# A state-space layer and its feed-forward part: part of the turns of x and the sum of squares leave TensorE

## The chip, the cores and the metric

The kernel runs on one core of a Trainium2 chip. The metric is the device time of one execution in microseconds (us); the lower the better. Its median over three runs is 1739.33 us.

## What is computed

The input is x, two sequences of 512 tokens with 512 features. A Mamba-2 layer and then a gated feed-forward layer with LoRA terms are added to it. What matters here is the scan of the first, which the reference runs in chunks (cut; the kernel takes chunks of 128 tokens and not of 32, with the same result):

```python
proj = input_states @ in_proj_w.T                     # gate, x, B, C, dt
xBC = silu(conv(xBC) + conv_b)                        # 4 taps along the tokens
scores = einsum('bcihn,bcjhn->bcijh', Cc, Bc) * Ldec * dtc
y_intra = einsum('bcijh,bcjhp->bcihp', scores, xc)
states = einsum('bcjh,bcjhn,bcjhp->bchpn', dtc * dlast, Bc, xc)
y_inter = einsum('bcihn,bchpn->bcihp', Cc * exp(cum), prev)
y = y_intra + y_inter + Dp * x
g = y * silu(gate)
gg = g.reshape(b, l, G, GS)                           # 8 groups of 1024 channels
var = mean(gg * gg, axis=-1)
g = (gg * rsqrt(var + EPS)).reshape(b, l, INTER) * norm_w
return g @ out_w.T
```

Two things of this are touched. `y_intra` and `states` sum over tokens, so they need x with the tokens on the partitions, while the projection leaves it with the channels there: x is turned. And `var` is a mean over 1024 channels, which lie on the partitions (8 tiles of 128), so its last step is a sum across partitions.

## The kernel before

It is written by hand for five engines, each with its own program and semaphores between them. There are 8 groups of 16 heads (1024 channels) and, in each, 8 chunks of 128 tokens (4 to a sequence): 64 slots, one for each group g and chunk k. K counts them, c = k mod 4 is the place in the sequence.

In one slot TensorE (PE) does, in this order: `inside` (L1788, decay times x, 32 matmuls); `square_total` (L1862, the sum of squares of the slot before, y times a column of ones); `new_state` (6 matmuls, on L1712 to L1714); the first projection tile of the next unit; `turn_x` (L1762, eight 128x128 transposes of x of the next chunk, through PSUM); `match` (L1771, L1772); `across` (L1803, 16 matmuls), which writes PSUM in which y of this chunk lies until DVE has gated it; two more tiles; `out_half`; a tile; `out_half`; the last tile. A tile of the projection is 12 matmuls of 512 columns (L1712 to L1714). Where c = 3 there is no new state and no `across`, and there are three tiles and not five.

VectorE (DVE) adds the skip to y (L1436), adds the new state (L1473, L1475), adds epsilon to the sum of squares (`mean_square`, L1481), gates (`gated`, L1449), runs the convolution's taps for finished tiles (L1385), scales x by dt out of PSUM into xdt (`scale_x`, L1404), accumulates the output of the slot before (L1487), scales `across` (L1425), and multiplies the scores (L1415). In slot k = 0 of a group it also makes the low halves of the output weights (`ow_low`, L1391). GpSimd (POOL) makes low halves (w_l L704, gT_l L738, xw_l L733), masks (L710), weighs x (`weigh_x`, L725), adds up squares within a partition (L744 to L748) and takes the inverse root (L753). ScalarE (ACT) drains, activates and squares. SyncE (SP) issues every DMA, in the order of its program, and waits where a buffer isn't free; all of them go to one queue.

What sets the order is the order in which each engine's program is written; nothing is scheduled. A PE matmul on a tile i waits until tile i - 2 has been drained and convolved, since two PSUM banks take turns. `scale_x` of the next chunk stands on DVE behind the gating and the first taps, and `accumulate` behind it.

```python
# DVE before
dve.wait_ge(ss_done, K + 1)
dve.tensor_scalar(mean_sq[:, :], total_of(K), EPS, None, ALU.add).then_inc(mean_ready, 1)
# PE, across
pe.wait_ge(g_half, K)
pe.wait_ge(state_ready, n_state(g, k))
```

## Time and profile before

| what | value |
|---|---|
| median of three runs | 1739.33 us (1739.27 to 1741.21) |
| span of the profiled execution, first to last instruction | 1737.2 us |
| granted TensorE clock over it | 0.999 of full speed |
| PE busy | 1724.5 us, 99% |
| DVE busy | 1221.0 us, 70% |
| ACT busy | 1192.8 us, 69% |
| POOL busy | 1182.1 us, 68% |
| DMA | 211.63 MB, queue of SP 41.7% of 16 engines' span |

The profile lists the span of its execution; the time around it is not listed apart, and the median run is 2.1 us above the span. A span is the time from the first to the last instruction; busy time is the time in which an engine computes. An average over the span hides that the slots differ: those with c = 3 take 17 us, the others 25.6 us, and DVE is nearly full in the first two slots of a group.

### The profile page before, as it was taken

The page shows a single profiled execution, that of the slowest core. Times are in us where ns is not written, and L with a number is a line of the kernel's source. Part 1 is how long each engine was busy: PE and PEld are TensorE (multiplying, and loading weights), DVE is VectorE, ACT ScalarE, POOL GpSimd, SP SyncE. Part 2 cuts the span into 40 slices and gives each one's busy share as a digit, 9 for nine tenths or more (in the row PEclk, how much of TensorE's full clock was granted, in tenths as well). Part 3 has the DMA queues.
Part 4 walks back from the last instruction along what each step waited for, and adds up shares of the span by engine and source line. Part 5 has one row for each costly group of instructions (what it writes and reads, how often), then busy time and mean ns, then how long its engine had stood idle before and what let it go on. Part 6 is the DMA issues. An engine that isn't in the chain of part 4 may idle for free.

```text
span 1737.2 us, 27735 instructions
## 1 busy us (share of the span) xinstructions
PE 1724.5 (99%) x9925; PEld 1436.9 (83%) x9925; DVE 1221.0 (70%) x2154; ACT 1192.8 (69%) x2232; POOL 1182.1 (68%) x1058
## 2 busy tenths in 40 slices
PE   9999999999999999999999999999999999999999
PEld 7788888888888888888888888888888888787887
DVE  8886778768785769676875878586867688663323
ACT  6887677767867677767776777768777777663421
POOL 5586768677777668676867687766867686774510
PEclk9999999999999999999999999999999999999999
DMA  5534435343543443443534354345343353444201
GB/s 192 171 107 116 125 116 169 109 119 105 162 128 114 121 146 112 121 116 112 174 115 115 97 162 128 114 122 151 114 118 113 110 174 101 118 114 134 80 15 49
DMA packets 122056, 211.63 MB, mean 122 GB/s; under 512 B 24256, under 2 KB 28992, under 8 KB 121920
## 3 DMA queue, kind: packets, MB, share of 16 engines
q1 hardware_dynamic: 121920, 209.87, 41.7%
q8 instruction: 80, 1.31, 0.3%
q14 instruction: 56, 0.46, 0.1%
HBM read 205.09 MB, written 4.72 MB: 121 GB/s over the span
## 4 chain that ended last, share of the span: by engine, by line
PE 97%; DVE 1%; DMA 1%; POOL 0%; ACT 0%; issue 0%; POOLq 0%
PE bank L1712 19%; PE bank L1714 18%; PE bank L1713 18%; PE bank L1788 7%; PE bank L1846 7%; PE bank L1836 7%; PE bank L1829 7%; PE bank L1803 5%; PE bank L1762 2%; PE bank L2091 1%; PE bank L2092 1%; PE bank L2093 1%; PE bank L1862 1%; PE bank L1772 1%; PE bank L1953 1%; DMA w_raw<-in_wp 0%
## 5 line engine op out<-in xcount | busy, mean ns | idle before, releaser
L704 POOL TENSOR_TENSOR w_l<-w_raw,w_h 128x512 fp32r<-128x512 f32 x288 | 379.6, 1321 | 341.2 <-ACT w_h L900 341.2
L1712 PE MATMUL bank<-x_h,w_h 128*128 128x512 f32 (+1 forms) x1328 | 527.0, 397 | 3.9 <-DVE x_ch L1385 2.3
L1714 PE MATMUL bank<-x_h,w_l 128*128 128x512 f32 (+1 forms) x1328 | 519.7, 391 | 0.0
L1713 PE MATMUL bank<-x_l,w_h 128*128 128x512 f32 (+1 forms) x1328 | 518.1, 390 | 0.0
L1385 DVE SCALAR_TENSOR_TENSOR x_ch<-bank,par,x_ch 128x511 f32<-128x511 f32 (+2 forms) x384 | 287.2, 749 | 80.3 <-ACT x_ch L918 71.2
L953 ACT ACTIVATE decay<-decay,cols 128x128 f32<-128x128 f32 x1024 | 318.2, 390 | 3.7 <-DMA cdec<-cdec_scratch 1.6
L1712 PEld LDWEIGHTS bank<-x_h,w_h 128*128 128x128 f32 (+1 forms) x1328 | 249.5, 188 | 55.1 <-issue 3.1
L1714 PEld LDWEIGHTS bank<-x_h,w_l 128*128 128x128 f32 (+1 forms) x1328 | 249.2, 188 | 54.6
L1713 PEld LDWEIGHTS bank<-x_l,w_h 128*128 128x128 f32 (+1 forms) x1328 | 249.7, 188 | 51.1
L1415 DVE TENSOR_TENSOR decay<-decay,bank 128x512 f32<-128x512 f32 x256 | 171.3, 683 | 107.1 <-ACT decay L953 107.1
L918 ACT ACTIVATE x_ch<-bank,par 128x512 f32<-128x512 f32 x128 | 99.0, 774 | 185.6 <-PE bank L1714 185.5
L710 POOL TENSOR_SCALAR_AFFINE_SELECT decay<-decay 128x512 f32<-128x512 f32 x256 | 173.9, 697 | 65.8 <-DMA decay<-cum_scratch 64.3
L1436 DVE SCALAR_TENSOR_TENSOR bank<-x_ch,par,bank 128x128 f32<-128x128 f32 x512 | 138.4, 350 | 92.8 <-PE bank L1788 92.8
L900 ACT ACTIVATE w_h<-w_raw 128x512 fp32r<-128x512 f32 x288 | 178.7, 621 | 4.4 <-DMA w_raw<-in_wp 4.4
L738 POOL TENSOR_TENSOR gT_l<-sgT,gT_h 128x1024 fp32r<-128x1024 f32 x64 | 153.9, 2405 | 8.2 <-ACT gT_h L972 8.2
L939 ACT ACTIVATE sgT<-bank 128x512 f32<-128x512 f32 x122 | 71.9, 590 | 111.9 <-PE bank L1714 111.7
L1846 PE MATMUL bank<-ow_h,gT_h 128*128 128x512 f32 x512 | 137.3, 390 | 0.0
L1836 PE MATMUL bank<-ow_h,gT_l 128*128 128x512 f32 x512 | 136.9, 389 | 0.0
L1829 PE MATMUL bank<-ow_l,gT_h 128*128 128x512 f32 x512 | 136.9, 389 | 0.0
L1788 PEld LDWEIGHTS bank<-decay,xdt 128*64 128x64 f32 x2048 | 110.5, 137 | 22.6 <-issue 22.6
L1788 PE MATMUL bank<-decay,xdt 128*64 128x128 f32 x2048 | 125.9, 276 | 0.0
L733 POOL TENSOR_TENSOR xw_l<-xw,xw_h 128x1024 fp32r<-128x1024 f32 x48 | 114.9, 2394 | 0.3 <-ACT xw_h L965 0.3
(161 smaller groups left out, 2760.0 us busy)
## 6 DMA issues: line engine op xcount, KB each, us to landing
w_raw<-in_wp SPq DMA_DIRECT2D x288, 256.0 KB, 3.0
decay<-cum_scratch SPq DMA_DIRECT2D x256, 256.0 KB, 4.1
ec<-ecum_scratch SPq DMA_DIRECT2D x96, 256.0 KB, 6.2
ow_raw<-in_ow SPq DMA_DIRECT2D x64, 256.0 KB, 4.8
w_raw<-in_w SPq DMA_DIRECT2D x48, 256.0 KB, 2.7
acc<-in_x SPq DMA_DIRECT2D x8, 256.0 KB, 4.5
out<-acc SPq DMA_DIRECT2D x8, 256.0 KB, 2.0
cols<-cols_scratch SPq DMA_DIRECT2D x16, 96.0 KB, 2.7
```

Of the source, the lines that this page charges most:

```text
L704: pool.tensor_tensor(w_l[:, s, :], w_raw[:, s, :], w_h[:, s, :].bitcast(F32), ALU.subtract).then_inc(wl_ready, 1)
L710: pool.affine_select(out=d, in_=d, compare_op=ALU.is_ge, fill=fill, base=0, pattern=[[0, QH], [1, P]], channel_multiplier=-1).then_inc(mas ...
L900: act.activation(w_h[:, s, :], w_raw[:, s, :], ACT.Copy).then_inc(wh_ready, 1)
L953: last = act.activation(decay[:, h, :], decay[:, h, :], ACT.Exp, bias=cols[:, b, CUM, c, h:h + 1], scale=-1.0)
L1385: dve.scalar_tensor_tensor(out=conv(bu, t)[:, s:], in0=bank_of(u, i)[:, 0:SEQ - s], scalar=w, in1=conv(bu, t)[:, s:], op0=ALU.mult, op1=AL ...
L1712: pe.matmul(dst, wh, xh, start=(opens and k == 0), stop=False)
L1713: pe.matmul(dst, wh, xl, start=False, stop=False)
L1714: last = pe.matmul(dst, wl, xh, start=False, stop=(k == len(terms) - 1 and not more))
L1788: last = pe.matmul(yb[n // 4][a * HDIM:(a + 1) * HDIM, tok(n % 4)], xdt[:, h * HDIM:(h + 1) * HDIM], decay[:, h, :], start=(c == 0), stop= ...
L1829: last = pe.matmul(ob[:, :], gT_h[:, n, :], ow_l[:, n, :], start=False, stop=(k == 0 and n == CT - 1))
L1836: last = pe.matmul(ob[:, :], gT_l[:, n, :], ow_h[:, n, :], start=False, stop=(k > 0 and n == CT - 1))
L1846: pe.matmul(ob[:, :], gT_h[:, n, :], ow_h[:, n, :], start=(n == 0), stop=False)
```

## The change

For chunks with c > 0 (three in four) PE no longer turns x. DVE turns it in 32x32 blocks into a spare buffer (`ec_sq` for c = 1, `xw_sq` for c = 2 and 3, in the space of ec and xw). Four DMAs put the blocks in their places in a scratch in DRAM (`store_x`), and one brings the turned chunk back into `x_rows` (`fetch_x`), in the space of gT_l. DVE's turns stand in slots c = 1 (for c = 3) and c = 3 (for c = 2 and c = 1 of the next unit). `scale_x` then reads `x_rows` in SBUF. Since `x_rows` lies under gT_l, POOL's gT_l waits for `scale_x`; since `xw_sq` lies under xw, POOL's `weigh_x` waits for the store. The fetch is the first DMA of its slot (behind par, cols and cdec where c = 0).

The sum of squares no longer goes to PE. At the head of the next slot DVE turns the 128x128 partial squares in blocks, sums each block over its 32 columns, and turns the 128x32 result (`turn_squares`); four DMAs of 4 rows of 128 bytes move it from SBUF to SBUF (`move_squares`, behind the second decay load); DVE turns what has arrived, sums 4 values and adds epsilon (`mean_square`), now behind `gated` and not ahead of it.

```diff
 def scale_x(g, k):                                   # DVE
-    dve.wait_ge(tx_done, K + 1)
+    if c > 0:
+        dve.wait_ge(x_fetched, 16 * moved_no(K))
+    else:
+        dve.wait_ge(tx_done, K // SC + 1)
...
+    xs = x_rows.rearrange("p (a s n t) -> p a n s t", a=2, s=QUADS // 2, n=CT)
...
+        last = dve.tensor_tensor(xd[:, a, :, :, :], xs[:, a, :, :, :], by, ALU.mult)
+def turn_x(g, k):                                    # DVE
...
+    dve.transpose(x_sq_of(k).rearrange("p b n t -> p n b t"), x_ch[:, b, :, tok(c)]).then_inc(x_turned, 1)
 def mean_square(g, k):                               # DVE
-    dve.wait_ge(ss_done, K + 1)
-    dve.tensor_scalar(mean_sq[:, :], total_of(K), EPS, None, ALU.add).then_inc(mean_ready, 1)
+    dve.wait_ge(sq_moved, 16 * QUADS * (K + 1))
+    dve.transpose(sq_back[:, :], sq_full[:, :]).then_inc(mean_step, 1)
+    dve.wait_ge(mean_step, 2 * K + 1)
+    dve.tensor_reduce(mean_sq[:, :], sq_back[:, 0:QUADS], mybir.AxisListType.X, ALU.add).then_inc(mean_step, 1)
+    dve.wait_ge(mean_step, 2 * K + 2)
+    dve.tensor_scalar(mean_sq[:, :], mean_sq[:, :], EPS, None, ALU.add).then_inc(mean_ready, 1)
+def turn_squares(g, k):                              # DVE
+    dve.wait_ge(sum_ready, K + 1)
+    dve.transpose(y[:, 1, :], y[:, 0, :]).then_inc(sq_turned, 1)
+    dve.wait_ge(sq_turned, K + 1)
+    dve.tensor_reduce(sq_part[:, 0:QUADS], y[:, 1, :].rearrange("p (b t) -> p b t", b=QUADS), ...)
+    dve.wait_ge(sq_summed, K + 1)
+    if some(K):
+        dve.wait_ge(sq_moved, 16 * QUADS * K)
+    dve.transpose(sq_rows[:, :], sq_part[:, :]).then_inc(sq_flipped, 1)
+def store_x(g, k):                                   # SP
+    sp.wait_ge(x_turned, turned_no(K))
+    for q in range(QUADS):
+        sp.dma_start(dst[q], x_sq_of(k)[q * SQ:(q + 1) * SQ, :, :, :]...).then_inc(x_stored[K % 2], 16)
+def fetch_x(g, k):                                   # SP
+    sp.wait_ge(x_stored[K % 2], stored_no(K))
+    if some(K - 1):
+        sp.wait_ge(out_done, 2 * (K - 1))
+    sp.dma_start(x_rows[:, :], xt_dram[K % 2]).then_inc(x_fetched, 16)
+def move_squares(g, k):                              # SP
+    sp.wait_ge(sq_flipped, K + 1)
+    if some(K):
+        sp.wait_ge(mean_ready, K)
+    for q in range(QUADS):
+        sp.dma_start(sq_full[q:P:SQ, :], sq_rows[q * SQ:q * SQ + QUADS, :]).then_inc(sq_moved, 16)
 def weigh_x(g, k):                                   # POOL
+    if c == 2:
+        pool.wait_ge(x_stored[1], stored_no(K + 1))
...
+    elif c == 0 and some(K):
+        pool.wait_ge(x_stored[0], stored_no(K + 2))
 def gT_low(g, k):                                    # POOL
+    if c < SC - 1:
+        pool.wait_ge(xdt_ready, K + 2)
-def square_total(g, k):                              # PE
-    pe.wait_ge(sum_ready, K + 1)
-    pe.matmul(total_of(K), y[:, 0, :], ones[:, :], start=True, stop=True).then_inc(ss_done, 1)
```

On DVE, at the start of slot k = 0 of a group, the order before is this (ow_l are the output weights' low halves, xdt is what `scale_x` writes, sgT what `gated` writes):

```order
L1436 SCALAR_TENSOR_TENSOR bank<-x_ch,par,bank 128x128 x8
L1475 COPY state<-bank 128x512 x2
L1481 TENSOR_SCALAR mean_sq<-bank 128x1
L1449 TENSOR_TENSOR sgT<-bank,sgT 128x4x128 x2
L1391 SCALAR_TENSOR_TENSOR ow_l<-ow_raw,par,ow_h 128x512 x2
L1404 TENSOR_TENSOR xdt<-bank,cols 128x512 x2
L1487 SCALAR_TENSOR_TENSOR acc<-bank,rstd,acc 128x512
```

And after the change, from the same place:

```order
L1607 STREAM_TRANSPOSE y<-y 128x128
L1609 TENSOR_REDUCE sq_part<-y 128x4
L1614 STREAM_TRANSPOSE sq_rows<-sq_part 128x32
L1552 SCALAR_TENSOR_TENSOR bank<-x_ch,par,bank 128x128 x8
L1591 COPY state<-bank 128x512 x2
L1565 TENSOR_TENSOR sgT<-bank,sgT 128x4x128 x2
L1597 STREAM_TRANSPOSE sq_back<-sq_full 128x32
L1599 TENSOR_REDUCE mean_sq<-sq_back 128x1
L1601 TENSOR_SCALAR mean_sq<-mean_sq 128x1
L1483 SCALAR_TENSOR_TENSOR ow_l<-ow_raw,par,ow_h 128x512 x2
L1509 TENSOR_TENSOR xdt<-x_rows,cols 128x8x64 x2
L1620 SCALAR_TENSOR_TENSOR acc<-bank,rstd,acc 128x512
```

Three instructions stand ahead of the skip (L1552), and three in place of one behind the gating; the ow_l, the scaling of x and the accumulation are queued behind them.

On SP, at the start of slot k = 0 of a group, before:

```order
L472 DMA par<-in_par 128x66
L475 DMA cols<-cols_scratch 128x192
L476 DMA cdec<-cdec_scratch 128x64
L455 DMA w_raw<-in_wp 128x512
L469 DMA ow_raw<-in_ow 128x512 x2
L481 DMA decay<-cum_scratch 128x512 x4
L487 DMA ec<-ecum_scratch 64x1024 x2
```

And after:

```order
L501 DMA par<-in_par 128x66
L504 DMA cols<-cols_scratch 128x192
L505 DMA cdec<-cdec_scratch 128x64
L534 DMA x_rows<-xt_scratch 128x1024
L484 DMA w_raw<-in_wp 128x512
L498 DMA ow_raw<-in_ow 128x512 x2
L510 DMA decay<-cum_scratch 128x512 x2
L545 DMA sq_full<-sq_rows 4x32 x4
L510 DMA decay<-cum_scratch 128x512 x2
L516 DMA ec<-ecum_scratch 64x1024 x2
```

The fetch of 512 KB stands ahead of the weights and decays, and the four moves of squares between the second and third decay load.

## Rows read from the trace of the kernel before

**Rows 1.** The page: busy time of the engines

```profile
PE 1724.5 (99%) x9925; PEld 1436.9 (83%) x9925; DVE 1221.0 (70%) x2154; ACT 1192.8 (69%) x2232; POOL 1182.1 (68%) x1058
```

**Rows 2.** Windows, slots 0, 1, 5 of group 4: PE, PEld, DVE, ACT, POOL

```profile
828.00:853.60 25.60, 25.60 (x154) 21.51 (x153) 23.15 (x35) 20.97 (x42) 21.76 (x17) 1.00 0.61 190
853.60:879.20 25.60, 25.60 (x154) 21.51 (x153) 22.74 (x40) 19.43 (x35) 20.91 (x18) 1.00 0.41 114
947.40:973.00 25.60, 25.60 (x152) 21.52 (x151) 20.81 (x36) 17.29 (x34) 18.31 (x16) 1.00 0.45 114
```

**Rows 3.** Timeline, DVE, slots 0, 1 and 3

```profile
834.26 1.41 DVE L1391 SCALAR_TENSOR_TENSOR ow_l<-ow_raw,par,ow_h 128x512 fp32r<-128x512 f32 x2
835.58 1.28 DVE L1404 TENSOR_TENSOR xdt<-bank,cols 128x512 f32<-128x512 f32 x2
837.62 0.75 DVE L1487 SCALAR_TENSOR_TENSOR acc<-bank,rstd,acc 128x512 f32<-128x512 f32 x1 [0.75 <-POOL rstd L753]
838.28 5.28 DVE L1391 SCALAR_TENSOR_TENSOR ow_l<-ow_raw,par,ow_h 128x512 fp32r<-128x512 f32 x4
...
855.84 2.16 DVE L1436 SCALAR_TENSOR_TENSOR bank<-x_ch,par,bank 128x128 f32<-128x128 f32 x8
...
859.16 1.28 DVE L1449 TENSOR_TENSOR sgT<-bank,sgT 128x512 f32<-128x512 f32 x2
...
908.14 1.29 DVE L1449 TENSOR_TENSOR sgT<-bank,sgT 128x512 f32<-128x512 f32 x2
```

**Rows 4.** Timeline, PE, slots 1 and 4: start us, length us

```profile
855.48 0.38 PE L1862 MATMUL bank<-ones,y 128*128 128x1 f32 x2
855.72 0.48 PE L1712 MATMUL bank<-xw_h,b_tok_h 128*128 128x512 f32 x1
...
859.94 0.80 PE L1762 MATMUL bank<-ident_r,x_chr 128*128 128x128 f32 x8
860.57 0.25 PE L1771 MATMUL bank<-ident_r,bcTr 128*128 128x128 f32 x1
...
860.95 1.95 PE L1803 MATMUL bank<-bcT,state 128*128 128x128 f32 x16
...
923.96 0.48 PE L1712 MATMUL bank<-xw_h,b_tok_h 128*128 128x512 f32 x1
```

**Rows 5.** Groups by line: busy us, mean ns of one

```profile
L1762 PE MATMUL bank<-ident_r,x_chr 128*128 128x128 f32 x512 | 51.1, 244 | 0.0
...
L1458 DVE TENSOR_TENSOR state<-state,cdec 128x1024 f32<-128x1024 f32 x32 | 46.2, 1445 | 0.0
...
L1412 DVE TENSOR_TENSOR b_tok_l<-bank,b_tok_h 128x128 fp32r<-128x128 f32 x64 | 18.0, 281 | 0.0
```

**Rows 6.** Timeline, decay loads issued by SP, slots 0 and 3

```profile
830.60 2.16 SPq L481 DMA_DIRECT2D decay<-cum_scratch  x4
...
905.49 1.75 SPq L481 DMA_DIRECT2D decay<-cum_scratch  x4
```

**Rows 7.** DMA issues, window 830.55 to 831.05 us

```profile
decay<-cum_scratch SPq DMA_DIRECT2D x1, 256.0 KB, 5.2
```

**Rows 8.** DMA issues, window 831.05 to 831.5 us

```profile
decay<-cum_scratch SPq DMA_DIRECT2D x1, 256.0 KB, 5.4
```

**Rows 9.** DMA issues, window 914.0 to 914.3 us

```profile
par<-in_par SPq DMA_DIRECT2D x1, 33.0 KB, 2.5
```

**Rows 10.** DMA issues, window 828.65 to 828.9 us

```profile
cdec<-cdec_scratch SPq DMA_DIRECT2D x1, 32.0 KB, 4.5
```

**Rows 11.** DMA issues of the whole span

```profile
ecum_scratch<-x_ch SPq DMA_DIRECT2D x4, 128.0 KB, 3.4
...
cdec_scratch<-cdecT SPq DMA_DIRECT2D x2, 2.0 KB, 3.7
```

**Rows 12.** Timeline, POOL, slot 3

```profile
916.51 1.91 POOL L725 TENSOR_TENSOR xw<-xdt,cols 128x1024 f32<-128x1024 f32 x1
...
921.00 2.38 POOL L733 TENSOR_TENSOR xw_l<-xw,xw_h 128x1024 fp32r<-128x1024 f32 x1
```

More of the change, by code:

```diff
@@ L33 @@
 PIECE = KT * P
+SQ = 32
+QUADS = P // SQ
 SLOT_TILES = [[("g", 0), ("g", 1), ("c", 0), ("c", 1), ("g", 2)],
@@ L129, in build @@
     cols_dram = nc.dram_tensor("cols_scratch", (GROUPS, BATCH, P, UNIT_COLS), F32, kind="Internal").ap()
+    xt_dram = nc.dram_tensor("xt_scratch", (2, P, GCH), F32, kind="Internal").ap()
     cdec_dram = nc.dram_tensor("cdec_scratch", (BATCH, GROUPS, GH * SC), F32, kind="Internal").ap()
@@ L174, in build @@
         decay = sc("decay", [P, GH, P])
+        ec_sq = under("ec_sq", [P, QUADS, CT, SQ])
         ec = sc("ec", [P, CT, P])
@@ L178, in build @@
         xw = under("xw", [P, GCH])
+        xw_sq = under("xw_sq", [P, QUADS, CT, SQ])
         xw_l = sc("xw_l", [P, GCH], F32R)
@@ L182, in build @@
         y_r = sc("y_r", [P, CT, P], F32R)
-        gT_h, gT_l = sc("gT_h", [P, CT, P], F32R), sc("gT_l", [P, CT, P], F32R)
+        gT_h = sc("gT_h", [P, CT, P], F32R)
+        x_rows = under("x_rows", [P, GCH])
+        gT_l = sc("gT_l", [P, CT, P], F32R)
         b_tok_h, b_tok_l = sc("b_tok_h", [P, P], F32R), sc("b_tok_l", [P, P], F32R)
@@ L326, in build @@
         tx_done = sem("tx_done")
+        x_turned = sem("x_turned")
+        x_stored = [sem(f"x_stored{n}") for n in range(2)]
+        x_fetched = sem("x_fetched")
         mt_done = sem("mt_done")
@@ L644, in body @@
                             load_decay(gn, kn, q)
+                            if q == 1 and some(K):
+                                move_squares(*before)
+                    if c == 0:
+                        sp.wait_ge(x_stored[1], stored_no(K + 1))
                     if more and kn % SC > 0:
@@ L655, in body @@
                         load_next_w(g, last, b, tiles[0])
+                    if c == 1 or first:
+                        store_x(g, k + 2)
+                    if c == SC - 1:
+                        store_x(gn, kn + 2)
                     if k == 0 and not first:
@@ L724, in weigh_x @@
                     pool.wait_ge(cols_stored[1], 32)
+                if c == 2:
+                    pool.wait_ge(x_stored[1], stored_no(K + 1))
+                elif c == 1 and not some(K - 1):
+                    pool.wait_ge(x_stored[0], stored_no(K + 1))
+                elif c == 0 and some(K):
+                    pool.wait_ge(x_stored[0], stored_no(K + 2))
                 pool.tensor_tensor(per_head(xw[:, :]), per_head(xdt[:, :]), spread(cols[:, b, ELAST, c, :], HDIM),
@@ L1402, in scale_x @@
                         dve.wait_ge(xw_ready, n_state(*((g, k) if k else (g - 1, CHUNKS))))
-                for h in range(2):
-                    last = dve.tensor_tensor(per_head(xdt[:, half(h)]), per_head(xt[h][:, :]),
-                                             spread(cols[:, b, DT, c, h * 8:h * 8 + 8], HDIM), ALU.mult)
-                last.then_inc(xdt_ready, 1)
+                if c == 0:
+                    for h in range(2):
+                        last = dve.tensor_tensor(per_head(xdt[:, half(h)]), per_head(xt[h][:, :]),
+                                                 spread(cols[:, b, DT, c, h * 8:h * 8 + 8], HDIM), ALU.mult)
+                    last.then_inc(xdt_ready, 1)
+                    return
+                xs = x_rows.rearrange("p (a s n t) -> p a n s t", a=2, s=QUADS // 2, n=CT)
+                xd = xdt.rearrange("p (n a s t) -> p a n s t", n=CT, a=2, s=QUADS // 2)
+                dts = cols[:, b, DT, c, :].rearrange("p (n a) -> p a n", a=2)
+                for a in range(2):
+                    by = dts[:, a, :].unsqueeze(2).unsqueeze(3).broadcast_to([P, CT, QUADS // 2, SQ])
+                    last = dve.tensor_tensor(xd[:, a, :, :, :], xs[:, a, :, :, :], by, ALU.mult)
+                last.then_inc(xdt_ready, 1)
+            def turn_x(g, k):
+                K, b, c = g * CHUNKS + k, k // SC, k % SC
+                dve.wait_ge(silu_done, conv_no(2 * g + b, CONV_TILES))
+                if c == 1 and some(K - 1):
+                    dve.wait_ge(z_scaled, n_across(g, k))
+                if c == 2:
+                    dve.wait_ge(st_done, n_state(g, k - 2) if some(K - 2) else 1)
+                if c == SC - 1:
+                    dve.wait_ge(st_done, n_state(g, k - 1))
+                dve.transpose(x_sq_of(k).rearrange("p b n t -> p n b t"), x_ch[:, b, :, tok(c)]).then_inc(x_turned, 1)
             def scores(g, k, q):
@@ L1583, in last_chunk @@
                 add_state(LAST, k)
+                gated(LAST, k)
                 mean_square(LAST, k - 1)
-                gated(LAST, k)
+                if k == SC + 1:
+                    turn_x(LAST, k + 2)
                 if k < CHUNKS - 1:
@@ L1630, in body @@
                         norm_apply(1, 1)
+                    if not first:
+                        turn_squares(*before)
                     if k != 1:
@@ L1639, in body @@
                         add_state(g, k)
+                        gated(g, k)
                         mean_square(*before)
-                        gated(g, k)
+                    if c == 1 or first:
+                        turn_x(g, k + 2)
+                    if c == SC - 1:
+                        turn_x(gn, kn + 2)
                     if late:
@@ L2028, in body @@
                         projects(tiles[2:3])
-                    if not first:
-                        square_total(*((g, k - 1) if k else (g - 1, CHUNKS - 1)))
                     new_state(g, k)
```

89 lines of the change are left out of this document (66 added, 23 removed).

## The prediction

> **What bounds the kernel now.** I read the page first. PE is busy for 1724.5 of 1737.2 us [rows 1], so the time is what PE has to do, and what leaves PE is a gain as long as nothing new makes it wait. Then the windows over slots of group 4, in mid-kernel, which show how much room the others have. In slot 0 of group 4, PE works 25.60 of 25.60 us at full granted clock (1.00, the 2.4 GHz level), DVE 23.15 and POOL 21.76; in slot 1 DVE 22.74 [rows 2]. In the fullest of the other slots, slot 5, DVE works 20.81. So the reader should look at DVE in the first two slots of a group: 5.3 us are free in two slots of 51.2 us, and the change gives DVE work there and takes time from PE there. The timeline of DVE in these slots [rows 3] shows that the room isn't where it would help: between the accumulation at 837.62 and the skip at 855.84 no row of it has an idle time.
>
> **What leaves PE.** Eight transposes of x take from 859.94 to 860.57, when the next kind of matmul begins: 0.63 us [rows 4]. There are 512 of them before [rows 5], 64 chunks of 8; three chunks in four leave, so 48 x 0.63 = 30.2 us. The sum of squares is one matmul in two passes for each of 64 chunks; from its start at 855.48 to that of the next matmul at 855.72 are 0.24 us [rows 4], and without it the next one starts in its place: 64 x 0.24 = 15.4 us. Together 45.6 us, which is the floor: 1739.3 - 45.6 = 1693.7 us.
>
> **What DVE gets.** The trace has no block transpose and no such reduction. The turn of x (128x1024) makes 1024 elements a partition, like the fading of the state, which takes 1.445 us in the mean with POOL beside it [rows 5]; a 128x512 one takes 0.64 (half of the 1.28 of the pair at 835.58 [rows 3]). I take 1.25 us, since one input is lighter than two; the bounds are 0.65 and 1.45. Turning the 128x128 squares I put at the 0.28 us of the 128x128 subtraction [rows 5], the reduction the same, the small turn at 0.15: 0.75 us at the head of each slot with what lies between them (bounds 0.4 and 0.85). The three small ones of `mean_square` I put at 0.5 us where there was one of 0.15 (bounds 0.3 and 0.85, three times the 0.28). `scale_x` from SBUF I leave at its 1.28 us (below for the other case). In the slots k = 2, 4, 5, 6 all this fits: the store and the fetch lie a slot ahead of their use, and DVE has at least the 4.8 us of slot 5 free there [rows 2]. There PE keeps the whole gain.
>
> **Where it doesn't fit: slot 0 and slot 1.** `mean_square` now waits for four tiny DMAs, and DVE waits in order, with ow_l, `scale_x`, `accumulate` and all of the slot behind it. When do these rows land? SP issues the decay loads of slot 0 from 830.60 on [rows 6]. The first lands after 5.2 us, at 835.8 [rows 7], the second, issued at 831.1, after 5.4, at 836.5 [rows 8], though a load alone lands far sooner: par, 33 KB, takes 2.5 us at 914.1 [rows 9]. What delays it is what stands ahead in the queue, and a small transfer isn't spared: cdec, 32 KB, took 4.5 us behind four loads of output weights [rows 10]. The moves are issued behind the second decay load, so they land behind it. The fetch, 512 KB, is now ahead of all: two times the 0.7 us between the two decay landings, 1.4 us. So the squares are there at 836.5 + 1.4 = 837.9, say 838.0.
>
> By the Trainium skill (DMA: Bandwidth & Descriptors, Queues, rings and completion order) each DMA engine works through the descriptors of a ring in ring order, so rows of 128 bytes stand behind the 256 KB loads on the engines that they use; the trace agrees, by cdec above.
>
> From 838.0: `mean_square` to 838.5; two ow_l, 1.41 [rows 3], to 839.9; `scale_x`, 1.28, to 841.2. `accumulate`, which began at 837.62, begins at 841.2: 3.6 us late. DVE then runs without a gap to the skip of slot 1, at 855.84 before, and three new instructions (0.75) stand ahead of it. So gating comes 4.35 us late. Its first half ended at 859.16 + 0.64 = 859.80 [rows 3]; it ends at 864.15. `across` waits for that half. It began at 860.95 [rows 4]; with two turns and two sums gone from the two slots, 1.74 us, it could begin at 859.2. PE therefore loses 4.95, say 5.0 us in slots 0 and 1 together. Part of it will show earlier, at the last tile of slot 0 (which waits for taps that now come 3.6 us late) and at gT_l, which waits for `scale_x`; these are the same 5.0 us, not more of them. Behind the gating the order holds: gated, `mean_square`, turn, taps end at 864.8 + 0.5 + 1.25 + 2.3 = 868.9, which is just when PE wants that bank. Seven groups have such a slot 0 (group 0 has no squares to move in it): 7 x 5.0 = 35 us. In slot 1 of group 0 DVE is as full; I put 1 us there.
>
> **Slots 3 and 7.** `weigh_x` there waits for the store of the turned c = 2. Gating ends at 908.14 + 1.29 = 909.4 [rows 3]. The decays are issued from 905.49, 0.44 us each [rows 6], so the last move goes out at about 907.7 and lands, at the 2.5 us of par in a quiet queue [rows 9], at 910.2. `mean_square` to 910.7, turn to 911.95, the last of four stores out at 913.3. A store of 128 KB lands in 3.4 us [rows 11]: 916.7, where `weigh_x` began at 916.51. Then squares and xw_l follow on POOL, which ended at 923.38 [rows 12] for a `new_state` that began at 923.96 [rows 4] and would now begin at 923.48. So of the 0.2 us about 0.1 to 0.2 shows, in 15 such slots 2 to 3 us; I take 3.
>
> **The sum.** 45.6 - 35 - 1 - 3 = 6.6 us gained. The profiled span of 1737.2 would be 1730.6, and the median of the runs, 2.1 us above that span, 1739.3 - 6.6 = 1732.7: I say 1733 us. A change can be told from none here from about 0.2%, 3.5 us, so this is a small gain, 0.4%. Its own range: with the fetch hidden (moves land at 836.5) the term of 35 falls by 7 x 1.4 = 10, to 1723; with the small instructions at their upper bounds (0.1 and 0.35 more on the path of 7 slots, the turn 0.2) it grows by 4.5, and with late stores by some more, to 1742.
>
> **Rivals.** *First, faster: the moved rows aren't held up.* They then land 2.5 us after the last issue, 833.3: 835.8. `mean_square` to 836.3, ow_l 837.7, `scale_x` 839.0: 1.4 us late, with the squares 2.15, `across` loses 2.75, 19 us in seven groups: 1739.3 - 45.6 + 19 + 4 = 1717 us. For it: the moves touch 16 rows in all, and that so small a transfer waits as cdec did isn't shown for them. Against it: cdec itself. If DVE catches up by shorter instructions too, the way leads on towards the floor, 1694. Chance 0.22.
>
> *Second, slower: the store of slots 3 and 7 is late.* If the moves take the 3.7 us of the 2 KB store of cdec [rows 11] and not 2.5, everything behind them in that slot is 1.2 us later, and the store lands at 917.9: `weigh_x`, xw_l and `new_state` are 1.4 us late, less the 0.1 of room, 15 x 1.3 = 20 us, in place of the 3: 1750 us. Every further microsecond (the store took 3.4 in a head with little traffic) costs 15 more. It turns the gain into a loss from 0.45 us of mean lateness above what I took. For it: DVE, SP, DMA and POOL stand in one row with no room in it. Against it: it needs both landings at their longer values. Chance 0.22.
>
> *Third, no change: `scale_x` from SBUF is slower.* Two ow_l at 834.26 take 1.41 us, four at 838.28 take 5.28, 1.32 each [rows 3]: the first while POOL waits, the others beside POOL's gT_l and masks. The new `scale_x` has both inputs in SBUF as they have, and may take 2.6 and not 1.28. In slot 0 that is 1.3 us more on the path, 7 x 1.3 = 9 us: 1742 us. Against it: in slot 0 POOL has nothing to do just then, since gT_l waits for this very instruction. Chance 0.14.
>
> The Trainium skill has this as a rule (VectorE: DVE Perf Modes, Two Vector instructions with no wait between them): what a Vector instruction with two SBUF inputs reads through the second SBUF read interface is shared with GpSimd. The trace agrees by the 1.32 against 0.70 us of the same instruction.
>
> **How the numbers follow.** The forecast's case has 0.42, of which 0.27 lies under 1735.8, 0.10 within 3.5 us of before and 0.05 above. The first rival is all faster (0.22), the second all slower (0.22), the third half within and half above (0.07 each). Faster: 0.27 + 0.22 = 0.49; same: 0.10 + 0.07 = 0.17; slower: 0.05 + 0.22 + 0.07 = 0.34. The range reaches into both outer rivals, from 1704 to 1755, and leaves 0.1 out on each side.
>
> **What would show it.** In the profile after: PE's rows have no L1762 in three chunks of four and 5.7 us less work a group; where my sum holds, a group takes about as long as before less 1 us, slots 2, 4, 5, 6 are 24.7 us, and slots 0 and 1 together 54.5 us less the gain they have in them, 1.74, plus 5.0, that is about 3.3 us longer than their 51.2. PE waits in them for DVE's taps and gating. On DVE in slot 0 there is an idle time of about 4 us ahead of the new `mean_square`, put down to the DMA of sq_full, and its landing is 6 us or so behind its issue. In the first rival this idle time is under 2 us. In the second, `weigh_x` in slots 3 and 7 waits for the DMA on xt_scratch and `new_state` for xw_l. In the third the pair of `scale_x` takes over 2 us. I would be most wrong if PE hardly waited anywhere, or if every slot waited for its squares and not slot 0 alone.

## The result, and the profile after

The changed kernel took 1757.97 us in the median (1754.29 to 1760.57, 4 runs), the kernel before 1739.3 (1739.09 to 1741.21, 4 runs): ratio 1.0104, interval 1.0092 to 1.0116. It is 18.7 us slower. The forecast was 1733, range 1704 to 1755, so it was wrong in sign and the time lies outside its range. The profiled run took 1760.57 us, with a span of 1758.8.

The engines' busy times on the page of the changed kernel:

```profile
PE 1697.5 (97%) x9413; PEld 1395.6 (79%) x9413; DVE 1363.7 (78%) x2524; ACT 1195.8 (68%) x2232; POOL 1203.4 (68%) x1058
```

PE works 27 us less than in [rows 1] and yet the span is 21.6 us longer: it was idle for 12.7 us of its span before, and for 61.3 now. DVE works 143 us more. The windows over slots 0, 1 and 5 of group 4 (columns as in [rows 2]) show where:

```profile
836.39:866.37 29.98, 27.23 (x142) 21.35 (x142) 24.18 (x41) 21.45 (x42) 22.26 (x17) 0.94 0.58 174
866.37:892.16 25.79, 25.01 (x143) 20.63 (x142) 24.52 (x48) 18.74 (x34) 20.96 (x18) 1.00 0.56 173
958.28:982.95 24.67, 24.67 (x144) 20.62 (x143) 22.79 (x43) 17.21 (x34) 18.68 (x16) 1.00 0.55 161
```

Slot 5 is 24.67 us, 0.94 less than before, with PE busy throughout; so are slots 2, 5 and 6 of groups 0 to 6, and their slots 3 and 7 are 16.78. Slot 0 is 29.98. A slot here runs from the start of one `inside` on PE to the next. Over groups 1 to 7 slot 0 has 30.06 us in the mean and slot 1 25.57: together 6.3 us above two slots of 24.67. Slots 0 and 1 of one group are called a pair below.

DVE in slot 0 of group 4, its timeline (start us, length us, line, operation, in brackets the idle time ahead and what ended it), with one row of POOL at the end:

```profile
841.37 1.28 DVE L1565 TENSOR_TENSOR sgT<-bank,sgT 128x512 f32<-128x512 f32 x2
847.47 0.21 DVE L1597 STREAM_TRANSPOSE sq_back<-sq_full 128x32 f32<-128x32 f32 x1 [4.83 <-DMA sq_full<-sq_rows]
...
847.98 1.40 DVE L1483 SCALAR_TENSOR_TENSOR ow_l<-ow_raw,par,ow_h 128x512 fp32r<-128x512 f32 x2
849.30 1.28 DVE L1509 TENSOR_TENSOR xdt<-x_rows,cols 128x512 f32<-128x512 f32 x2
850.51 0.74 DVE L1620 SCALAR_TENSOR_TENSOR acc<-bank,rstd,acc 128x512 f32<-128x512 f32 x1
...
850.74 2.37 POOL L828 TENSOR_TENSOR gT_l<-sgT,gT_h 128x1024 fp32r<-128x1024 f32 x1 [1.61 <-DVE xdt L1509]
```

And PE in the same slot, the three rows that have an idle time ahead, and the window from 853.50 to 857.00:

```profile
851.35 1.17 PE L1996 MATMUL bank<-ow_h,gT_h 128*128 128x512 f32 x4 [0.90 <-issue]
853.16 1.81 PE L1986 MATMUL bank<-ow_h,gT_l 128*128 128x512 f32 x4 [0.64 <-POOL gT_l L828]
...
860.72 0.47 PE L1861 MATMUL bank<-x_h,w_h 128*128 128x512 f32 x1 [1.06 <-DVE bcT L1477]
```

```profile
853.50:857.00 3.50, 3.50 (x10) 2.48 (x9) 3.50 (x5) 2.81 (x8) 3.50 (x4) 0.51 0.02 7
```

DVE stands for 4.83 us in front of the moved squares, 11.1 us into the slot; `scale_x`, `accumulate` and, on POOL, gT_l come behind, and PE waits three times. After the first two waits the granted clock is 0.51 for 3.5 us, the lower level of 1.2 GHz, and four matmuls on ow_l take 2.06 us at 854.77, where four of the same size take 1.07 in slots without a wait. This isn't so in every pair: the clock fell in those of groups 1, 3 and 4 and stayed at 1.00 in the other four, whose waits are much the same.

Over the seven pairs PE is idle for 29.7 us. Most of it, by what ended it: 13.3 us the convolved tile bcT (DVE's taps, late in slot 0), 4.3 gT_l, 4.1 ahead of the first matmul of `out_half` (listed as "issue"; in the six pairs where it has an idle time it begins 0.10 us after `accumulate` ends, for which the program makes it wait), 3.9 `gated` in slot 1 and 2.4 ow_l.

Two stalls stand outside the seven pairs. In slot 0 of group 0, PE:

```profile
103.81 2.07 PE L1986 MATMUL bank<-ow_h,gT_l 128*128 128x512 f32 x4 [6.50 <-POOL gT_l L828]
```

And POOL, which waits for the `scale_x` that DVE begins at 99.64, behind the taps of bcT and the turn of x:

```profile
101.04 2.71 POOL L828 TENSOR_TENSOR gT_l<-sgT,gT_h 128x1024 fp32r<-128x1024 f32 x1 [11.40 <-DVE xdt L1509]
```

And in the last group from slot 3 to slot 4, one row each of SP, DVE, POOL and PE:

```profile
1497.66 2.20 SPq L545 DMA_DIRECT2D sq_full<-sq_rows  x4
...
1505.44 0.21 DVE L1597 STREAM_TRANSPOSE sq_back<-sq_full 128x32 f32<-128x32 f32 x1 [5.63 <-DMA sq_full<-sq_rows]
...
1506.11 0.55 POOL L843 TENSOR_TENSOR rstd<-mean_sq,minus_half 128x1 f32<-128x1 f32 x1 [7.31 <-DVE mean_sq L1601]
...
1509.07 0.77 PE L1861 MATMUL bank<-xw_h,b_tok_h 128*128 128x512 f32 x1 [8.55 <-POOL xw_l L821]
```

By slot lengths the account is: 49.0 us saved (48 x 0.70 + 64 x 0.24); 7 x 6.3 = 44 lost in the pairs, 9.8 in the first slot (29.01 us where 19.91 less 0.70 was due), 1.5 in the slot behind it, 10.5 in slot 4 of the last group (40.26 us against 29.31 of the two behind it; 30.7 against 30.22 before). Of the two large ones the waits are 6.50 and 8.55; behind each the granted clock is 0.50, for 5.57 us from 103.81 on and for 3.19 from 1509.07 on, which at half speed is 2.8 and 1.6 us more (an estimate from these lengths). Then 1737.2 - 49.0 + 44 + 9.8 + 1.5 + 10.5 = 1754, against a span of 1758.8. Of the rest about 2 us are slots 4, 0.3 us above 24.67 in the mean, and 2.2 are a later end of the head, which lay anywhere from 81.8 to 85.8 us in the profiles of the kernels below and which I don't put down to the change.

### The profile page after: what moved, and what is told of

Same layout as the page of the kernel before. It is cut to its first block, busy times and chain, and to the rows that moved or that the text cites. A ratio compares the mean times of both kernels' runs of the same rounds, so it can differ in the third digit from the quotient of the medians.

```text
span 1758.8 us, 27765 instructions
## 1 busy us (share of the span) xinstructions
PE 1697.5 (97%) x9413; PEld 1395.6 (79%) x9413; DVE 1363.7 (78%) x2524; ACT 1195.8 (68%) x2232; POOL 1203.4 (68%) x1058
## 3 DMA queue, kind: packets, MB, share of 16 engines
q8 instruction: 76, 1.25, 0.3%
## 4 chain that ended last, share of the span: by engine, by line
PE 79%; DVE 10%; SPq 4%; DMA 4%; issue 2%; ACT 1%; POOL 1%; DVEq 0%; POOLq 0%
PE bank L1861 16%; PE bank L1862 15%; PE bank L1863 15%; PE bank L1986 5%; PE bank L1979 5%; PE bank L1996 5%; PE bank L1937 5%; PE bank L1952 4%; DVE ow_l L1483 3%; DMA sq_full<-sq_rows 2%; DVE bcT L1477 1%; PE bank L2226 1%; PE bank L2227 1%; PE bank L2225 1%; SPq L498 1%
## 5 line engine op out<-in xcount | busy, mean ns | idle before, releaser
L1861 PE MATMUL bank<-x_h,w_h 128*128 128x512 f32 (+1 forms) x1328 | 529.9, 399 | 17.6 <-DVE bcT L1477 13.3
L792 POOL TENSOR_SCALAR_AFFINE_SELECT decay<-decay 128x512 f32<-128x512 f32 x256 | 191.2, 764 | 56.1 <-DMA decay<-cum_scratch 54.3
L1552 DVE SCALAR_TENSOR_TENSOR bank<-x_ch,par,bank 128x128 f32<-128x128 f32 x512 | 137.8, 347 | 33.9 <-PE bank L1937 33.7
L1986 PEld LDWEIGHTS bank<-ow_h,gT_l 128*128 128x128 f32 x512 | 96.3, 189 | 33.8 <-POOL gT_l L828 14.2
```

The costliest lines, as they stand in the source:

```text
L792: pool.affine_select(out=d, in_=d, compare_op=ALU.is_ge, fill=fill, base=0, pattern=[[0, QH], [1, P]], channel_multiplier=-1).then_inc(mas ...
L1861: pe.matmul(dst, wh, xh, start=(opens and k == 0), stop=False)
L1986: last = pe.matmul(ob[:, :], gT_l[:, n, :], ow_h[:, n, :], start=False, stop=(k > 0 and n == CT - 1))
```

## The experiments

All kernels are timed against the kernel before on the same chip, whose median was 1737.4 to 1739.7 us; ratios are to it.

**One part alone.** `x_only`: x turned by DVE with its store and fetch, the squares by TensorE as before. The edit in short (it stands in many places, here named by its functions):

```diff
-                turn_squares(...) / move_squares(...) / mean from sq_back
+                square_total(...) on PE, mean from total_of(K)      # as before
```

> This kernel keeps the turn of x by DVE with its stores and fetches, and gives the sum of squares back to TensorE as before. Theory 1 (the moved squares, for which DVE waits in order, are the cost; the turn of x is nearly free): 1739.3 less 48 turns of 0.70 us (33.6) plus the first slot, which is 9.7 late behind the turn of x and the taps, plus 1.4 in the slot after it and 2.2 in the head: about 1719 us, with slots 0 of groups 1 to 7 back at 25 us. Theory 2 (the round trip of x through memory is what makes slot 0 long, since gT_l shares its space with the fetched x): slots 0 of groups 1 to 7 stay at 29 us or more and the time is 1740 us or more.

Measured 1727.49 us (1725.71 to 1728.75), ratio 0.9933 (0.9917 to 0.995). Slots 0 are 26.02 in the mean and slots 1 25.08, where the others are 24.91. So the turn of x is worth 0.70 us a slot, and the pairs lose 1.3 and not 6.3; slot 0 of group 0 is still 28.73. The time lies between the two theories, nearer the first, which had the pairs at no loss: 7 x 1.3 = 9 us is about its miss.

`sq_only`: the squares by DVE and moved rows, x turned by TensorE as before. In short again:

```diff
-                store_x(...) / fetch_x(...) / turn_x(...) on DVE, scale_x from x_rows
+                turn_x(...) on PE in every slot, scale_x from the bank   # as before
```

> This kernel keeps the sum of squares by DVE turns and moved rows, and gives the turn of x back to TensorE as before (no store, no fetch). Theory 1: 1739.3 less 15.4 (64 x 0.24), plus slots 0 of seven groups late by 3 to 6 us each, since the moves still stand behind the four ow loads, the weights and two decay loads but no longer behind the 512 KB fetch, plus 8 to 10 in the last group: 1765 us, 1752 to 1775. Theory 2 (the squares are harmless without the fetch of x ahead of them): 1724 to 1732 us.

Measured 1741.3 us (1738.75 to 1746.0), ratio 1.0014 (1.0003 to 1.0025). Slots 2, 5 and 6 are 25.37, so the 0.24 us a slot is there; pairs lose 1.6 us, slot 4 of the last group is 4.7 above the two behind it (34.72 against 29.99; 0.5 before). I had expected 1765: DVE's wait in slot 0 of group 4 is 2.18 us here, and little of it reaches PE. One part is 12.2 us faster, the other 1.6 slower (medians against that of before in the same runs), both together 18.7 slower: 29 us come from having both. Of these the pairs have 7 x (6.3 - 1.3 - 1.6) = 24. The last group has 5: its slot 4 lies 10.95 us above those behind it in the changed kernel, 1.54 in `x_only` (31.08 against 29.54), 4.73 in `sq_only` and 0.48 before, so it loses 10.47 against 1.06 and 4.25.

**What holds up the moves.** `sq_before_fetch`: in slot 0 of groups 1 to 7 the moves are issued ahead of the fetch and all loads.

```diff
+                    if k == 0 and some(K):
+                        move_squares(*before)
                     if c < SC - 1:
                         fetch_x(gn, kn)
...
-                            if q == 1 and some(K):
+                            if q == 1 and k > 0:
                                 move_squares(*before)
```

> The changed kernel with one edit: in slot 0 of groups 1 to 7 SP issues the four moves of the squares ahead of the fetch of x, the weights, the two ow loads and the decay loads, and not behind them. Theory 1 (the moves are late because they stand behind 2.3 MB of loads that were issued first): DVE no longer waits 4.8 us ahead of mean_square, slots 0 fall from 30.1 to about 25 us and the pairs by about 6 us each: 1757 less 38 to 43, so 1717 us. Rival (a move of 128-byte rows takes 5 us or more from its issue whatever stands ahead, or the fetch that now comes 2 us later holds scale_x up by as much): 1750 us or more.

Measured 1740.11 us (1736.66 to 1742.85), ratio 1.0005 (0.9995 to 1.0014). DVE doesn't wait, as its timeline in slot 0 of group 4 shows, and the windows over slots 0 and 1 show what is left:

```profile
832.14 1.28 DVE L1567 TENSOR_TENSOR sgT<-bank,sgT 128x512 f32<-128x512 f32 x2
833.34 0.20 DVE L1599 STREAM_TRANSPOSE sq_back<-sq_full 128x32 f32<-128x32 f32 x1
```

```profile
827.20:853.31 26.11, 24.93 (x142) 20.54 (x141) 25.15 (x41) 21.69 (x42) 22.45 (x17) 1.00 0.69 202
853.31:879.16 25.85, 25.03 (x142) 20.65 (x141) 24.78 (x49) 18.94 (x35) 21.00 (x18) 1.00 0.58 171
```

In the seven pairs the wait and the low clock are gone and 18 us with them, half of what I had expected. The pairs still have 52.62 us, 3.3 above 49.34: DVE now works 49.9 of 52.0 us in these two slots, and PE waits there for what DVE writes, 1.06 us for bcT at 847.71 and 0.79 for `gated` at 860.80. DVE's own work, in its order, is the limit there.

`fetch_after` puts only the fetch (512 KB) behind the moves, `bulk_after` only the weight tile and two ow loads (768 KB):

```diff
                                 move_squares(*before)
+                                if k == 0:
+                                    fetch_x(gn, kn)          # fetch_after
+                                    load_next_w(...); load_ow(g, ...)  # bulk_after
```

> The changed kernel with the fetch of x, 512 KB, behind the moves of the squares in slot 0 of groups 1 to 7, and the weights, ow and decay loads still ahead of them. Theory (the moves wait for the bytes that are queued ahead): they land about 1.4 us earlier (512 KB at the 0.65 us that each 256 KB takes in the row of landings), but the fetch lands some 3 us later and holds scale_x and gT_l; nothing to 10 us gained of the 18 that all loads behind the moves gave, 1748 to 1758. Rival (it is the fetch and it alone that holds the moves up): the full 18 us, 1740.

> The changed kernel with the weight tile and the two ow loads, 768 KB, behind the moves in slot 0 of groups 1 to 7, and the fetch of x still ahead of them. Theory (bytes queued ahead, whichever they are): issued 1.4 us earlier and with 2 us less ahead of them the moves land 2.0 to 3.4 us earlier, DVE's wait of 4.8 us falls to 1.5 to 3, and the kernel gains 10 to 18 us: 1740 to 1748. Rival (only the fetch counts): 1756 or more.

Measured 1746.49 us, ratio 1.0045 (1.0029 to 1.006), and 1746.37 us, ratio 1.0046 (1.003 to 1.0062); each is 10 to 12 us under the changed kernel (by ratios and by medians). `bulk_after` lies where it was expected and `fetch_after` 1.5 us under its range; both rivals fall. DVE in slot 0 of group 4, first of `fetch_after`, then of `bulk_after`:

```profile
835.78 0.21 DVE L1599 STREAM_TRANSPOSE sq_back<-sq_full 128x32 f32<-128x32 f32 x1 [1.49 <-DMA sq_full<-sq_rows]
```

```profile
841.16 0.21 DVE L1597 STREAM_TRANSPOSE sq_back<-sq_full 128x32 f32<-128x32 f32 x1 [1.78 <-DMA sq_full<-sq_rows]
```

The wait falls from 4.83 to 1.49 and 1.78. It isn't the fetch of x as such: taking either load away from ahead of four moves of 0.5 KB brings them some 3 us forward. Both edits also issue the moves earlier. The slots 0 of groups 1 to 6 tell the two apart (means, us; from the end of SP's fourth issue to DVE's first row on the squares):

| kernel | fourth move issued, into the slot | squares on DVE, into the slot | between them |
|---|---|---|---|
| changed | 6.76 | 10.69 | 3.93 |
| `fetch_after` | 5.56 | 8.26 | 2.70 |
| `bulk_after` | 4.37 | 7.81 | 3.44 |

With the fetch behind them the moves come 2.4 us earlier, half by their place in SP's row and half by what stands ahead in the queue; with the weights and ow loads behind them 2.9 us, of which 2.4 by their place.

**Is it the wait in order?** `mean_later`: moves as in the changed kernel, but in slot 0 `mean_square` behind two ow_l and `scale_x` on DVE, the inverse root behind gT_l on POOL (DVE's part of the edit is shown).

```diff
                     scale_x(gn, kn)
+                    if k == 0 and not first:
+                        mean_square(*before)
                     if not first:
                         accumulate(*before)
```

> The changed kernel with the moves as they are, but in slot 0 of groups 1 to 7 mean_square stands on DVE behind two ow_l and scale_x, and on POOL the inverse root stands behind gT_l. Theory 1 (what costs is not that the mean is late but that DVE and POOL wait for it in order, with scale_x and gT_l behind it): the mean lands at the same time, the accumulation about 1 us before TensorE asks for its bank, and the time falls by 30 to 42 us, to about 1720. Rival (the late mean itself holds TensorE through the accumulation, with scale_x hidden anyway): less than 10 us gained, 1748 us or more.

Measured 1768.1 us (1763.36 to 1769.93), ratio 1.0164 (1.0144 to 1.0183): 10 us slower than the changed kernel. That is in the rival's range (1748 or more), but its trace shows neither theory at work. Slot 0 of group 4, DVE with one row of POOL:

```profile
848.02 1.63 POOL L786 TENSOR_TENSOR w_l<-w_raw,w_h 128x512 fp32r<-128x512 f32 x1 [3.19 <-ACT w_h L992]
...
847.82 2.38 DVE L1511 TENSOR_TENSOR xdt<-x_rows,cols 128x512 f32<-128x512 f32 x2
...
853.37 0.75 DVE L1622 SCALAR_TENSOR_TENSOR acc<-bank,rstd,acc 128x512 f32<-128x512 f32 x1 [2.67 <-POOL rstd L843]
```

The wait for the squares went, but my edit made another: `accumulate` now waits 2.67 us for the root, which stands on POOL behind gT_l. And `scale_x` takes 2.38 us beside POOL's w_l, where it took 1.28 alone. DVE works 27.21 us in this slot, 24.18 in the changed kernel. The clock differs too: it was 0.50 for 30.7 us of the seven pairs, in all of them, against 10.2 us in three of the changed kernel. So the kernel doesn't settle what it was made for; it shows that here DVE's new wait and its longer instructions reached PE (which waits 4.00 us at once at 864.00, for bcT), and how much of the 10 us is clock stays open.

**The price of x in SBUF.** `x_scale_first` (below) scales the fetched rows; in `x_from_bank` all stays but `scale_x` reads a PSUM bank (and the matmuls that fill this bank next wait for it). This kernel leaves out the use of the turned x, so it only prices the read.

```diff
-                if c == 0:
+                if True:
                     for h in range(2):
                         last = dve.tensor_tensor(per_head(xdt[:, half(h)]), per_head(xt[h][:, :]), ...
```

> The kernel of the x turns with the first slot mended (1722), in which DVE turns, stores and fetches x as before, but scale_x reads the bank of the chunk state in place of the fetched rows (so the values scaled are not those of x; all instructions stay in number and place). It prices the reading of x from SBUF. Theory (an operation of DVE with both operands in SBUF takes longer while GpSimd works: 0.68 us alone, up to 1.79 beside it, and no such difference with an operand in PSUM): scale_x takes 0.68 us each throughout, DVE's 128 operations of scale_x sum to 88 and not 114 us, slots 0 shorten from 26.0 by up to 0.7 and slots 1 by up to 0.2, so the time falls by 3 to 6 us. Rival (the longer times come from where x lies or from the broadcast of three dimensions, not from GpSimd): no fall in the time of fewer than 2 us, or scale_x still over 0.7 us beside GpSimd.

Measured 1714.41 us (1712.8 to 1716.9), ratio 0.9861 (0.9846 to 0.9875), 7.8 under `x_scale_first` by the medians and 7.0 by the ratios, more than expected. The groups of `scale_x`, by form (busy us, mean ns of one), first of `x_scale_first`, then of `x_from_bank`:

```profile
L1503 DVE TENSOR_TENSOR xdt<-x_rows,cols 128x512 f32<-128x512 f32 x96 | 87.2, 950 | 0.0
L1494 DVE TENSOR_TENSOR xdt<-bank,cols 128x512 f32<-128x512 f32 x32 | 20.6, 686 | 4.2 <-PE bank L1886 2.6
```

```profile
L1494 DVE TENSOR_TENSOR xdt<-bank,cols 128x512 f32<-128x512 f32 x128 | 82.0, 682 | 4.5 <-PE bank L1886 2.5 <-DMA x_rows<-xt_scratch 0.4
```

From SBUF one takes 950 ns in the mean, from 648 to 1786, from the bank 682 (649 to 692), as before the change. Since the shortest from SBUF is as short, neither the place of x nor the form of the read makes it long by itself. Slots 0 fall from 26.04 to 25.16, 7 x 0.88 = 6.2 of the 7.8 us. That is a term that the forecast's sum had put at nothing. The Trainium skill's rule on the second SBUF read interface that Vector's two-input instructions share with GpSimd (VectorE: DVE Perf Modes, Two Vector instructions with no wait between them) agrees: 1.28 us for the pair while POOL waits, 2.38 beside it, and no such step with one input in PSUM.

**The two stalls outside the pairs.** `scale_first` changes slot 0 of group 0 alone, `sq_before_up` slot 3 of the last group alone:

```diff
                         add_state(g, k)
+                        scale_x(gn, kn)
+                        turn_x(g, k + 2)
                         taps_of(tiles[2:3])
...
+                        move_squares(g, k)
                         first_up()
-                        move_squares(g, k)
```

> The changed kernel with one edit, in its very first slot alone: DVE runs scale_x and the turn of x for slot 2 ahead of the taps of bcT and not behind them. Theory: the 9.7 us that this slot lost came from gT_l, which lies on the fetched x and so waits for scale_x; the fetched x landed at 92.1, so scale_x can run at about 92.9 in place of 99.6, gT_l is ready before TensorE asks, and the slot falls from 29.0 to 20 or 21 us: 1758 less 8, so about 1750. Rival (the slot is held by the landing of the four decay loads, 96.5 to 99.4, and their masks and exponentials, whatever DVE does): less than 3 us gained.

> The changed kernel with one edit, in slot 3 of the last group alone: SP issues the moves of the squares ahead of the LoRA and up weights (2.0 MB) and not behind them. Theory: slot 4 of the last group lost 10 us because DVE waited 5.6 us and POOL 7.3 us for the mean of squares, with xw_l and the skip behind; with the moves first the mean is there at 1500 and slot 4 falls from 40.3 to about 31: about 1749. Rival (the weights, the fetch and the decay loads that now come later hold the next two slots up as much; the kernel with the squares alone still had 34.7 there): 4 us or less gained, 1754 or more.

Measured 1754.46 us, ratio 1.0081 (1.0066 to 1.0096), and 1756.38, ratio 1.0102 (1.0081 to 1.0123). The first slot falls from 29.01 to 22.67 us, the slot in the last group from 40.26 to 35.35. Both causes are right where they were named, but the slots gave back 6.3 and 4.9 us and not 9 each, and the medians 3.5 and 1.6. The whole time alone would not show the second: its interval overlaps that of the changed kernel, and 1756 lies in the rival's range (1754 or more); for it the slot speaks, here and in `all_three`. The pairs vary from run to run: in the profile of `sq_before_up` one slot 0 is 33.39, and the granted clock fell in it twice.

`all_three` has the three edits of order together; `all_four` also runs xw_l ahead of the inverse root on POOL in slot 3 of the last group.

> The changed kernel with three edits of order: moves of squares ahead of the fetch in slot 0 of groups 1 to 7 (1740.1 alone), scale_x and turn ahead of the taps in the first slot, moves ahead of the up weights in the last group. Theory: the three stalls are apart in time and their gains add: 1740 less 8 less 9, so 1723. What is left to 1690 is then the first two slots of each group, where DVE's own work (25 us in 26) is the bound. Rival (the gains overlap or are given back): 1730 or more.

> All three edits of order together (1731.3), and in slot 3 of the last group POOL runs xw_l ahead of the inverse root and not behind it. Theory: slot 4 of the last group still had 35.9 us since TensorE waited 3.6 us for xw_l behind the root, which waits for the moved squares; it falls to 31 or 32 and the time to 1727. Rival (the 4 us come from something else in that slot): within 1 us of 1731.

Measured 1731.26 us, ratio 0.9951 (0.9933 to 0.9969), and 1728.3, ratio 0.9936 (0.9919 to 0.9952). So both parts can be in one kernel at a gain. `all_three` came out 8 us above its expectation, in its rival's range: the single gains were smaller than I had said, and part of the first slot's is given back in the slot behind it (21.70 for 28.95 us in `sq_before_fetch`, then 29.33 for 26.67). `all_four` took PE's wait for xw_l from 3.6 to 1.9 us, but its slot fell from 35.91 to 35.02 and not to 31 or 32; what holds the rest of it, 5.7 us above the two behind, wasn't looked for. The pairs are 53.0 and 52.8 us.

`x_scale_first` is `x_only` with the edit of the first slot.

> The kernel with the turn of x alone (1727.5, squares by TensorE as before) and the edit of the first slot. Theory: the 8.7 us of its first slot go too: 1719. If the first slot is held by something other than DVE's order, 1725 or more. It is also the candidate for the fastest version, against all three edits together.

Measured 1722.17 us (1721.0 to 1724.26), ratio 0.9901 (0.9887 to 0.9916); the first slot is 23.24, so 5.5 of its 9.5 us went, and the time lies between the two expectations (1719; 1725 or more).

**Squares only where DVE has time.** `hybrid`: x as in `x_scale_first`; 42 squares by DVE, 22 by TensorE.

```diff
+        def by_pe(K):
+            return K % CHUNKS in (0, CHUNKS - 1) or K >= (GROUPS - 1) * CHUNKS
```

> The kernel of the x turns with the first slot mended (1722), in which the squares are summed by DVE turns and moved rows for 42 of the 64 chunks alone: those whose sum falls in slots 2 to 7 of groups 0 to 6. The 22 others, whose sum falls in slots 0 and 1 or in the last group, where DVE has no time left, stay with TensorE. Theory (in slots 0 and 1 DVE's own work is the bound, 25 us in 26, and elsewhere TensorE's): 1722 less 42 x 0.24, so 1712, with slots 0 and 1 unchanged at 26.0 and 25.1 and slots 2, 5 and 6 at 24.7. Rival (the moves or the three short DVE operations cost what TensorE saves also in those slots): 1720 or more.

Measured 1740.08 us (1736.38 to 1747.35), ratio 1.001 (0.9997 to 1.0023), far from 1712. A row of PE says why, a wait of mine that had stayed from the kernel before:

```profile
888.66 0.25 PE L1940 MATMUL bank<-ident_r,bcTr 128*128 128x128 f32 x1 [0.69 <-DVE mean_sq L1614]
```

```diff
-                if some(K - 1):
+                if some(K - 1) and by_pe(K - 2):
                     pe.wait_ge(mean_ready, K - 1)
```

> The kernel of 42 squares by DVE and 22 by TensorE (1740.1), with one needless wait taken out: TensorE waited 32 times for the mean of the chunk before at the turn of B (0.5 us each in the trace, and the slots 2, 4, 5 and 6 stood at 25.33 and not at 24.67), a wait that guards the column of the bank into which TensorE sums squares, and which the chunks summed by DVE never use. Theory: slots 2, 4, 5, 6 of groups 0 to 6 fall to 24.67 and slots 3 and 7 to 16.8: 1740 less 28 x 0.66 less 14 x 0.2 less 3 for three longer slots, so 1715. Rival (DVE or the moves hold TensorE in those slots in another way): 1722 or more, no better than the squares by TensorE throughout.

`hybrid2` took 1718.17 us (1716.17 to 1719.05), ratio 0.9879 (0.9863 to 0.9895), between its expectation (1715) and its rival's (1722 or more), and the fastest here but for `x_from_bank`, which doesn't use the turned x. Slots 2, 5 and 6 of groups 0 to 6 are 24.67 and the pairs 51.58. Against `x_scale_first` it gains 4 us of the 10 that 42 x 0.24 makes; part of the rest is slots 0, 26.50 in the mean against 26.04. The two were timed apart and their intervals overlap a little, so the 4 us are less sure than the rest. The wait on PE, 0.5 us in each of 32 slots (16.0 us of idle time), had cost 22 us.

## Why the prediction was wrong, by its own steps

- **What leaves PE**: right. 45.6 us were forecast, 49.0 came: 48 x 0.70 and not 0.63, and 64 x 0.24 exactly. Slots 2, 5 and 6 are 24.67 us, as said.
- **What DVE gets**: right in the sizes of the new instructions. The turn takes 1.245 us (1.25 forecast), the three of the squares 0.30, 0.29 and 0.21 (0.75 in all), the three of the mean 0.21, 0.16 and 0.15 (0.5).
- **Where it doesn't fit**: right in place and mechanism, too small. The pairs lost 6.3 us, not 5.0: 44 and not 35. (The signs forecast both slots at 51.2 - 1.74 + 5.0 = 54.5 us; the 1.74 is already in the 54.5. 55.6 came.) The squares were back 11.1 us into the slot (10.0 forecast). The forecast had no time for the issue of the moves, which takes SP 0.55 us each, from 840.70 to 842.9. A lower granted clock, which no term held either, doesn't explain the rest: the pairs of groups 1, 3 and 4, in which it fell, take 55.5 us in the mean, the four others 55.8. In group 4 the lower level cost PE about 1.7 us (half of 3.5, an estimate), but it then waited 1.06 us for bcT where the six others waited 2.04; in groups 1 and 3 the wait of 0.8 us ahead of `across` in slot 1 is gone.
- **Group 0 was left out**: this step failed. I counted 1 us in slot 1 and nothing in slot 0, because no squares are moved there. But gT_l lies on the space of the fetched x and waits for `scale_x` in every slot, and in that slot `scale_x` stands behind taps that wait and behind a turn. 9.8 us; `scale_first` shows it and gives back 6.3.
- **The last group was left out**: this step failed as well. I read SP's order in the seven slots 0 and not in slot 3 of the last group, where the same moves stand behind `first_up` and POOL waits for them ahead of xw_l. 10.5 us, of which `sq_before_up` gives back 4.9 in the slot. In `sq_only`, without a fetch, the slot still lost 4.2.
- **Slots 3 and 7**: no loss, where 3 us were taken; both are 16.78 in groups 0 to 6, and the second rival (late stores) fell.
- **Third rival, `scale_x` from SBUF**: its mechanism is real, given a chance of 0.14 and held apart from the forecast. It costs 7 to 8 us in the kernel of the x turns alone. In the changed kernel's slot 0 the argument against it holds (1.28 at 849.30, POOL waits for it).
- **First rival, moves not held up**: false in the changed kernel. Its price was too good: with the moves out of the way (`sq_before_fetch`) the time was 1740 and not 1717, since the two stalls above stay and DVE is full in the pairs.

Forecast and result are 28 us apart in the profiled span: 9 from the pairs, 9.8 and 10.5 from the two stalls, against 3.4 more gain and 3 less loss in slots 3 and 7; some 5 are the small rests named above.

Without the two stalls the span would be 1738.5 us, about as before (1737.2): they made the loss, and the 9 us of the pairs had used up the gain that was forecast.

Not settled: PE's idle times say what ended each wait in the pairs, not what would be left if one of them went. The kernel that was to tell the way through gT_l from that through the accumulation made a wait of its own. Nor is it shown why the clock fell in three pairs and not in four.

## What to carry to other kernels

When an in-order engine gets a new wait, look for it in every place of the program where that step stands (first slot, last group, the slot before a change of phase), and not in the repeating one alone: two slots of 64 made 20 us of loss here. Tiny DMAs issued behind large loads were there 11.1 us into the slot here, and within 6.1 us when they were issued ahead of them; issue them first, or keep what waits for them away from the path. And work moved off the bound engine pays only in those stretches where its receiver has time: 42 squares moved gave 1718.2 us against 1722.2 with none (intervals that overlap a little), all 64 with every edit of order 1728.3.

## What the runs showed of the hardware that wasn't expected

- Short waits on PE can be followed by a stretch at the lower clock: in slot 0 of group 4 idle times of 0.90 and 0.64 us within 3 us, then 0.51 (1.2 GHz) over 3.5 us. They need not be: in group 5 idle times of 1.47, 0.65, 0.40 and 2.04 us in one slot left it at 1.00. The stretch around the idle time of 1.06 us at 860.72 is at 1.00 as well:

```profile
857.00:866.37 9.37, 8.31 (x36) 6.30 (x35) 9.30 (x13) 6.64 (x16) 9.21 (x8) 1.00 0.10 30
```

- A DVE operation with both tensors in SBUF ended 0.55 us after the operation that ran on GpSimd beside it. In `sq_before_fetch`, the first half of `scale_x` on DVE, and w_l on POOL, which ends at 836.39:

```profile
835.16 1.78 DVE L1511 TENSOR_TENSOR xdt<-x_rows,cols 128x512 f32<-128x512 f32 x1
...
834.86 1.53 POOL L788 TENSOR_TENSOR w_l<-w_raw,w_h 128x512 fp32r<-128x512 f32 x1 [3.16 <-ACT w_h L992]
```

It began 1.23 us before w_l ended and ended 0.55 us after it, 1.78 where the pair at 849.30 took 1.28 for both halves. In `mean_later` the second half of `scale_x` took 1.77 us and ended 0.55 us after w_l (850.20 and 849.65), and in the changed kernel an ow_l took 2.48 us and ended 0.54 us after gT_l (853.65 and 853.11). The turns (1.234 and 1.245 us in the mean) and `scale_x` from a bank (0.682) keep their length. The Trainium skill has the rule (SBUF — State Buffer, Who interferes with whom): the pair of ports that Vector shares with GpSimd is an exclusive lock, and a Vector instruction with two SBUF inputs contends with a GpSimd instruction that reads SBUF. These rows agree.
